# A Mamba and mixture-of-experts layer on one core: another distribution of gathers over steps, and one gate matmul two steps earlier

## The reference

```
# mamba, per batch: D_INNER = 256, D_STATE = 16
xz = rmsnorm(xn) @ in_proj.T ;  x_s, z = halves of xz
u  = silu(conv4(x_s)) ;  dt, B, C = split(u @ x_proj.T)
delta = softplus(dt @ dt_proj.T + dt_b)
h[t]  = exp(delta[t] * A) * h[t-1] + (delta*u)[t] * B[t]      # for each of 16 states
y = sum over states of h * C + u * D ;  y = y * silu(z)
mamba = y @ out_proj.T + xn
# moe: 8 experts, the best 2 of each token
moe = sum over the 2 chosen e of gate_e * (silu(xn @ w_gate[e]) * (xn @ w_up[e])) @ w_down[e]
```

## Time and profile before

| | |
|---|---|
| median of 3 runs | 620.43 us (619.95 to 621.5) |
| the profiled execution, its own time | 620.43 us |
| its span, first to last instruction | 618.6 us |
| busy DVE | 591.5 us, 96% |
| busy PE | 541.0 us, 87% |
| busy POOL | 509.0 us, 82% |
| busy ACT | 456.0 us, 74% |
| mean granted TensorE clock | 0.97 |

### The profile page before, as it was taken

The page is one execution under the profiler, slowest core; times in us unless marked ns, Lnnn a source line. Parts: engine busy times, 40 slices in busy tenths (PEclk is TensorE's granted clock), DMA queues, the critical chain, the costliest instruction groups (busy, mean ns, idle before and its releaser), DMA issues.

```text
span 618.6 us, 11479 instructions
## 1 busy us (share of the span) xinstructions
PE 541.0 (87%) x3554; PEld 421.7 (68%) x3554; DVE 591.5 (96%) x852; ACT 456.0 (74%) x916; POOL 509.0 (82%) x481
## 2 busy tenths in 40 slices
PE   5899888888988998999989899899999797778887
PEld 2367666656887777878788777887787465657564
DVE  6999959999999999999999999999999998999997
ACT  1799886139866798578886698767985679968881
POOL 5697159459999999998999989999998967885684
PEclk9899878979999999999999999999999899988999
DMA  7420209724877887878768788777984455333264
GB/s 215 143 105 1 73 1 195 291 76 175 275 242 260 265 271 258 303 240 293 263 225 299 261 270 288 243 266 264 296 271 159 153 174 224 110 97 105 64 146 91
DMA packets 60893, 122.99 MB, mean 199 GB/s; under 512 B 8218, under 2 KB 41378, under 8 KB 53794
## 3 DMA queue, kind: packets, MB, share of 16 engines
q1 hardware_dynamic: 53826, 112.42, 53.6%
q0 software_dynamic: 6288, 9.52, 7.2%
q10 hardware_dynamic: 720, 0.33, 0.3%
HBM read 112.77 MB, written 9.47 MB: 198 GB/s over the span
## 4 chain that ended last, share of the span: by engine, by line
PE 35%; DVE 20%; ACT 15%; issue 13%; POOL 13%; DMA 3%; DVEq 0%; ACTq 0%; POOLq 0%
DVE bank L1134 8%; POOL dbu L921 8%; PE bank L1421 6%; PE bank L1572 6%; DVE h_sb L1151 6%; PE bank L1586 4%; PE bank L1455 4%; ACT dbu L531 4%; PE bank L1580 4%; ACT da L503 3%; DMA xs<-xn_rows,src 2%; PE bank L1478 2%; POOL xs L908 2%; ACT bank L515 2%; PE bank L1384 2%
## 5 line engine op out<-in xcount | busy, mean ns | idle before, releaser
L921 POOL TENSOR_TENSOR dbu<-du,xn_all 128x512 f32<-128x512 f32 x172 | 215.4, 1275 | 21.1 <-DVE bank L1134 19.7
L1134 DVE TENSOR_TENSOR_SCAN bank<-bank,dbu 128x512 f32<-128x512 f32 x170 | 207.3, 1222 | 1.5 <-POOL dbu L921 0.5
L1151 DVE TENSOR_TENSOR h_sb<-bank,xh_all 128x512 f32<-128x512 f32 x240 | 158.8, 675 | 1.2
L515 ACT ACTIVATE bank<-delta,a_sb 128x512 f32<-128x512 f32 x170 | 116.7, 688 | 47.0 <-DVE h_sb L1151 44.0
L1421 PE MATMUL bank<-id_sb,h_sb 128*128 128x128 f32 x992 | 132.5, 277 | 12.2 <-DVE h_sb L1151 10.6
L1421 PEld LDWEIGHTS bank<-id_sb,h_sb 128*128 128x128 f32 x992 | 113.6, 143 | 23.5 <-DVE h_sb L1151 17.1
L1134 DVE TENSOR_TENSOR_SCAN bank<-da,bank 128x512 f32<-128x512 f32 x82 | 96.4, 1212 | 9.5 <-PE bank L1384 8.5
L1572 PEld LDWEIGHTS bank<-wd_sb,hid 117*128 117x128 f32 (+1 forms) x432 | 54.7, 190 | 49.7 <-DVE hid L1185 26.9
L1572 PE MATMUL bank<-wd_sb,hid 117*128 117x128 f32 (+1 forms) x432 | 64.1, 284 | 18.8 <-ACT xT L692 16.5
L908 POOL DMA_INDIRECT xs<-xn_rows,src x72 | 69.8, 970 | 12.5 <-issue 9.6
L531 ACT ACTIVATE dbu<-du_t,bc_sb 128x256 f32<-128x256 f32 x164 | 69.5, 497 | 10.8 <-PE bank L1384 7.8
(11 more groups left out here) (197 smaller groups left out, 894.5 us busy)
## 6 DMA issues: line engine op xcount, KB each, us to landing
xh_all<-b_rows SPq DMA_DIRECT2D x30, 1024.0 KB
xn_all<-b_rows SPq DMA_DIRECT2D x25, 1024.0 KB
wgu_sb<-in_w_gu SPq DMA_DIRECT2D x72, 352.0 KB
wd_sb<-in_w_dn SPq DMA_DIRECT2D x72, 192.0 KB
y_slots<-ys SPq DMA_DIRECT2D x72, 64.0 KB
xn_rows<-xn_all SPq DMA_DIRECT2D x2, 1040.0 KB, 11.4
out<-x_sb SPq DMA_DIRECT2D x7, 256.0 KB
x_sb<-in_x SPq DMA_DIRECT2D x2, 640.0 KB, 5.9
```

Of the source, the lines that this page charges most:

```text
L515: nc.scalar.activation(bank_of(b, m)[:, :], delta[b % 2][:, hf, :], ACT.Exp, scale=a_sb[:, hf, k:k + 1]).then_inc(s["da_rdy"], 1)
L921: nc.gpsimd.tensor_tensor(dbu[k % 2][:, hf, :], du[b % 2][:, hf, :], b_ring[c % 2][:, k % CH, :], ALU.mult).then_inc(s["dbu_p"], 1)
L1134: nc.vector.tensor_tensor_scan(at, da_of(n)[:, hf, :] if n in IN_SBUF else at, inp, 0.0, ALU.mult, ALU.add).then_inc(s["h_rdy"], 1)
L1151: nc.vector.tensor_tensor(h_sb[k % 2][:, hf, :], bank_of(b, 2 * k + hf)[:, :], row, ALU.mult).then_inc(s["p_rdy"], 1)
```

## The change

Two tables get other numbers. `EACH` has the gathers of batches 6 and 7 in other steps: counting the 3 of batch 5, 27 instead of 23 have been issued by the end of 6.10, 29 instead of 27 by the end of 6.12, 34 instead of 31 by the end of 6.14, and none is issued in 6.15; from 7.6 on up to two more than before. Their order among themselves is the same, and there are 64 as before. In `z_step`, the second half of z in batch 6 is named for step 9 instead of 11.

```
-                6: [1, 2, 2, 1, 2, 2, 2, 2, 2, 2, 2, 2, 2, 2, 2, 1],
-                7: [2, 2, 3, 2, 2, 3, 2, 2, 3, 2, 3, 2, 2, 2, 0, 0]}
+                6: [1, 1, 3, 1, 3, 3, 3, 2, 3, 2, 2, 1, 1, 2, 3, 0],
+                7: [2, 2, 2, 3, 2, 2, 3, 2, 2, 3, 2, 2, 2, 1, 0, 0]}
...
-            return {13: 1, 15: 0} if b == 0 else {7: 1, 11: 0} if b == 6 else {4: 1, 6: 0}
+            return {13: 1, 15: 0} if b == 0 else {7: 1, 9: 0} if b == 6 else {4: 1, 6: 0}
```

## The result

The changed kernel takes 624.56 us at the median of 8 runs (622.43 to 625.41), the kernel before 620.49 (8 runs). The ratio is 1.0054, with a 95% interval of 1.0036 to 1.0073: slower by about 3.3 us, beyond the upper end of the range (622.9). The forecast was 621.4, "within 0.3%".

The account below looks back on a forecast made before the run. DVE was taken as the bound, with ACT setting the pace in a piece of batch 6. DVE reaches 6.12 late by 1.6 (matmul) + 0.60 (product); less the swallowed wait and saved product, +1.0: 621.4 us, range 619.6 to 622.9.

Parts of the forecast that it names:

- The bound: Whole kernel: DVE busy for 96% of the span; in a piece of batch 6 ACT runs without a gap and DVE waits.
- z's matmul: PE's queue in 6.9: waits for DVE's first z product, delays DVE's second scan by 1.6 us (0.7 warm, 2.0 cold).
- z's tanh and product: ACT and DVE, moved from 6.12 to 6.10 under the wait before 6.12's scans: worth nothing alone, -0.03 us.
- The clock stays down and the queue behind runs late: Rival, PE's queue from 527.5 on: later work at 1.2 GHz delays DVE's 6.10 scan; +3.0 us, 623.4; chance 0.12.
- The better clock at the border: Rival "Faster", border of batches 6 and 7: lower clock falls elsewhere, saving up to about 0.9 us, 619.6; chance 0.11.
- `dbu` late: Rival, POOL at 7.0: additional gathers delay `dbu` beyond its 1.3 us cover; bound adds 1.2 us, 622.6; chance 0.03.
- POOL's gathers: no change: Step on the new `EACH` on POOL's queue: moved gathers delay nothing that DVE needs; 0.0 us, bounds -0.1 and +1.2.

Follow-up runs that it names:

- the sparse gathers: Full change, but with the old gathers up to step 6.8 and the missing ones made up in 6.10 to 6.13, against the kernel before: 1.0027.

## Why the prediction was wrong

**The bound.** That ACT sets the pace around 6.8 and DVE elsewhere is what the experiments rest on; the 1.42 us wait before the first z product is in every profile without the stop.

**z's matmul: right in mechanism and size.** Forecast were a start 4 us after PE went idle, the lower clock, a delay of 1.6 us of the second scan of 6.9 (0.7 if warm, 2.0 if cold throughout), the wait at 6.12 swallowed, and +1.0 us net. Measured where there was no stop: idle 4.00 us, wait 1.10, 1.77, 1.32, 1.33 and 1.40 us (1.95 with the sparse gathers, and 1.92 to 1.95 behind a stop), plus the 0.1 by which two scans overlap otherwise; 0.59 with PE kept warm; no wait at 6.12; batch 6 longer by 0.99, 1.16, 0.86, 0.84 and 0.84 us, 0.94 on the mean. The ratios of the z table, 1.0025, 1.0023 and 1.0024, say +1.5 us with intervals from 0.1 to 2.9 us; they agree with it and don't prove the 0.5 us above it.

**z's tanh and product: right.** With the matmul behind the accumulate, 6.12 waits 0.50 us instead of 0.61 and batch 6 is as long as before (61.81 against 61.87; -0.06, forecast -0.03).

**The rivals.** "The clock stays down and the queue behind runs late" didn't come: the accumulate of 6.8 took 1.91 us and the turn behind it 0.96 with the z table alone, but no later scan of batch 6 waited for them. The better clock at the border did come in the first profile: 0.18 us before the gate product instead of 0.97; the lower clock then fell later and took back 0.33 and 0.48 us in 7.2. "`dbu` late" didn't decide; the cover forecast was 1.3 us for it, and its first half was ready at 552.90 + 1.28 = 554.18, 1.36 us ahead of the scan.

**The step that failed: "POOL's gathers: no change", sum 0.0, bounds -0.1 and +1.2.** The working looked for instructions that wait for POOL, and for those behind a gather on POOL's queue ("What a gather can delay is what stands behind it on POOL's queue"). In half of the comparisons that was all. In the other half the new gather table comes with a stop of DVE of 2 us before 6.8. None of these waits explains it, since DVE waits there for PE's late signal. The net price of the stop in batch 6 is 1.47 us alone (63.34 - 61.87) and 1.1 on top of the matmul's wait (63.84 - 62.71), less than the stop itself, since the wait before the first z product is swallowed.

The first comparison's profiles add up as follows: 0.84 us for the matmul (62.71 - 61.87) and 1.13 for the stop in batch 6, -0.79 for the shorter wait before the gate product of 7.0, and +0.90 in batch 7 (57.74 - 56.84), where the two waits at the lower clock in 7.2 alone are 0.81. That is 2.1 us. The other 1.2 of the 3.3 us aren't located: the part ahead of 6.0, where the programs are the same, strays by more. Over the three full changes with the stop, batch 7 takes 57.74, 57.24 and 58.98 us, against 56.84 and 56.64 for the kernel before in two of these groups; the last has another stop of 1.97 us in 7.6.

The bounds were too narrow as well: an edit that moves 64 DMAs against the busiest engine was bounded by POOL's own timeline alone.

**Open.** Why PE's signals come late, and why the new gather table makes them late at 6.8. One thing goes with it: on POOL's queue the six gathers of steps 6.5 and 6.6 now follow each other at 0.3 us, where four did, and the late updates end soon after them (last gather over at 517.37 and update at 518.43 before; 521.69 and 523.00 in the change). That is a coincidence in time, not a cause shown. A different pace of POOL isn't it: its rows around the stop stand within 0.1 us at the same places in batch 6 in profiles with and without it. No run takes the gathers' density apart where the stop occurs: the kernel made for that came to a chip without it. Whether the late signals are bound to the chip or to something else that a group of runs shares is open too.

**The chances.** The forecast gave 0.14 to slower by over 0.3%. Of five comparisons of the full change, the three with the stop in the profile gave 1.0054, 1.0087 and 1.0049, the two without it 1.0029 and 1.0036. The intervals of 1.0054 and 1.0049 overlap those of the two, so the timings alone set only the 1.0087 apart; the profiles carry the difference. Even without the stop, slower by 0.3% was about as likely as within it: the matmul's wait alone should have had more chance on that side.

## What to carry to other kernels

A matmul with a late input, put at the head of a queue in which inputs for the busiest engine stand behind it, costs twice: by the order, and by the clock that the idle time takes away. Both can be read off before a run: look for the end of its input, for what stood there before, and for the idle time that results; if it must be early, let the inputs of the bound engine go first (here one position further back was enough), or fill the gap. When an engine stands still although its inputs are computed, look at the time of the semaphore update, not only at the end of the work that gives it. And an edit that only moves DMA issues on an idle enough engine isn't free until it was timed more than once and in more than one place: here seven profiles showed nothing, and five others a stop of 2 us.

## What the runs showed of the hardware

- After 4.00 to 4.65 us without a matmul PE was at 1.2 GHz by the end of the first pair of matmuls (z matmul 1.22 to 2.08 us instead of 1.02, the turn behind it 1.06 instead of 0.63), in each of the nine profiles with such a gap. With four double matmuls of 512 columns in the gap (3.60 us) it stayed at 2.4 GHz.
- In three of six groups of runs (the later five were on five different chips) some semaphore updates by PE are recorded late (at 6.8, 2.45 to 3.19 us after the turn whose result DVE needs), and DVE's scan starts 0.09 or 0.10 us behind them. With the new gather table this stops DVE for about 2 us before the scans of 6.8 (2.04, 1.99, 1.94, 2.08, and once 1.34 and 0.61). In batch 7 there are two more stops of this length (2.12 and 1.97), and 0.89 and 0.87 in the kernel before.
- The times of one program differ from run to run by more than the first runs let expect: the kernel before took 616.7 to 623.4 us over all its executions. In single profiles the beginning of batch 6 lies up to 4.5 us apart.
